# Two MLPs behind a gated linear recurrence on one core: splits and scans of the opening in another order, w_g and w_u split by ScalarE, b2 two rounds later

## What is computed

```python
t   = rmsnorm(x, norm1_w)
xb  = causal_depthwise_conv(t @ Wx, conv_w, conv_b)      # 4 taps
r, i = sigmoid(xb @ Wa), sigmoid(xb @ Wi)
a   = exp(-8 * softplus(lam) * r)
h_t = a_t * h_(t-1) + sqrt(max(1 - a_t**2, 1e-12)) * (i_t * xb_t)
h1  = x + (h * gelu(t @ Wy)) @ Wo
u   = rmsnorm(h1, norm2_w)
y   = h1 + (gelu(u @ Wg) * (u @ Wu)) @ Wd                # hidden size 1024
x1  = layernorm(x + y)
out = layernorm(x1 + relu(x1 @ W1 + b1) @ W2 + b2)       # hidden size 1024
```

## Time and profile before

| | us |
|---|---|
| three runs | 639.7, 638.1, 639.01; median 639.01 |
| profiled execution | 639.91 |
| its span, first to last instruction | 638.0 |
| TensorE busy | 606.2 (95%) |
| VectorE busy | 385.0 (60%) |
| ScalarE busy | 301.6 (47%) |
| GpSimd busy | 213.5 (33%) |
| HBM traffic | 15.7 MB, mean 25 GB/s |

### The profile page before, as it was taken

How to read it: one execution, slowest core, us unless ns; L and a number is a source line. 1 busy time by engine, 2 the same in 40 slices (tenths; PEclk the granted TensorE clock), 3 DMA queues, 4 the chain that set the end, 5 groups by cost and what they waited for, 6 DMA issues and landing times.

```text
span 638.0 us, 9412 instructions
## 1 busy us (share of the span) xinstructions
PE 606.2 (95%) x3621; PEld 538.6 (84%) x3621; DVE 385.0 (60%) x689; ACT 301.6 (47%) x560; POOL 213.5 (33%) x309
## 2 busy tenths in 40 slices
PE   8888788899999999999999999999999999999994
PEld 7787676778988888888988888888988889988884
DVE  3984883936467563857467563856467464653544
ACT  5665513427544564437544564437544563332341
POOL 4604326411353207341353207340353205420311
PEclk9989889979999999999999999999999999999998
DMA  8600000000000100001010100001000100010010
GB/s 267 219 2 33 1 2 1 33 0 2 2 34 0 34 1 14 21 1 34 1 34 1 34 1 9 25 1 34 2 1 1 34 1 1 1 34 2 0 34 33
DMA packets 13068, 15.68 MB, mean 25 GB/s; under 512 B 584, under 2 KB 12256, under 8 KB 13024
## 3 DMA queue, kind: packets, MB, share of 16 engines
q1 hardware_dynamic: 13024, 15.09, 7.0%
HBM read 10.89 MB, written 4.19 MB: 24 GB/s over the span
## 4 chain that ended last, share of the span: by engine, by line
PE 85%; DVE 8%; POOL 3%; issue 2%; ACT 1%; DMA 1%; POOLq 0%; ACTq 0%; DVEq 0%
PE psum L280 17%; PE psum L281 17%; PE psum L282 17%; PE psum L288 10%; PE psum L290 10%; PE psum L289 10%; PE psum L295 3%; DVE xb L720 1%; DVE gu_lo L822 1%; POOL rstd L999 1%; POOL normed L1030 1%; DVE tT_lo L709 1%; DMA xs<-in_L_attn_x_dram 1%; DVE gu_raw L817 0%; DVE x1T_lo L709 0%
## 5 line engine op out<-in xcount | busy, mean ns | idle before, releaser
L1059 POOL TENSOR_SCALAR gu_hi<-gu_raw 128x512 fp32r<-128x512 f32 x64 | 50.5, 790 | 299.2 <-DVE gu_raw L817 299.2
L827 DVE TENSOR_TENSOR hid_lo<-hid_raw,hid_hi 128x512 fp32r<-128x512 f32 x64 | 45.2, 707 | 95.1 <-ACT hid_hi L603 95.1
L599 ACT ACTIVATE hid_raw<-psum,vecs 128x512 f32<-128x512 f32 x64 | 43.9, 686 | 121.3 <-PE psum L282 121.3
L817 DVE TENSOR_TENSOR gu_raw<-psum,gu_raw 128x512 f32<-128x512 f32 x64 | 44.1, 689 | 92.7 <-PE psum L282 92.7
L590 ACT ACTIVATE gu_raw<-psum 128x512 f32<-128x512 f32 x64 | 38.3, 598 | 92.3 <-PE psum L282 91.7
L288 PE MATMUL psum<-w_d_hi,gu_hi 128*128 128x256 f32 x256 | 73.0, 285 | 5.9 <-DVE w_d_lo L838 3.5
L288 PE MATMUL psum<-w_hi,hid_hi 128*128 128x256 f32 x256 | 71.7, 280 | 1.2 <-DVE hid_lo L827 0.7
L290 PE MATMUL psum<-w_d_hi,gu_lo 128*128 128x256 f32 x256 | 72.2, 282 | 0.0
L289 PE MATMUL psum<-w_d_lo,gu_hi 128*128 128x256 f32 x256 | 72.0, 281 | 0.0
L290 PE MATMUL psum<-w_hi,hid_lo 128*128 128x256 f32 x256 | 71.8, 281 | 0.0
L289 PE MATMUL psum<-w_lo,hid_hi 128*128 128x256 f32 x256 | 71.7, 280 | 0.0
(11 more groups left out here) (145 smaller groups left out, 1548.8 us busy)
## 6 DMA issues: line engine op xcount, KB each, us to landing
xs<-in_L_attn_x_dram SPq DMA_DIRECT2D x8, 512.0 KB, 3.4
out_dram<-row SPq DMA_DIRECT2D x16, 256.0 KB, 2.2
raw<-in_L_ffn_W_dram SPq DMA_DIRECT2D x2, 1024.0 KB, 13.1
raw_gud<-in_L_attn_Wg_dram SPq DMA_DIRECT2D x1, 1024.0 KB, 9.0
raw_gud<-in_L_attn_Wu_dram SPq DMA_DIRECT2D x1, 1024.0 KB, 11.1
raw_gud<-in_L_attn_Wd_dram SPq DMA_DIRECT2D x1, 1024.0 KB, 13.2
raw_xyai<-in_L_attn_Wx_dram SPq DMA_DIRECT2D x1, 256.0 KB, 2.7
raw_xyai<-in_L_attn_Wy_dram SPq DMA_DIRECT2D x1, 256.0 KB, 3.1
```

Source lines behind the costliest of these rows:

```text
L599: nc.scalar.activation(hid_raw[:, w % SLOTS, :], bank[:, :], ACT.Relu, bias=vec("b1", m)).then_inc(relu_ready, 1)
L817: nc.vector.tensor_tensor(gu_raw[:, r % SLOTS, :], up_bank(r)[:, :], gu_raw[:, r % SLOTS, :], ALU.mult).then_inc(gu_ready, 1)
L827: nc.vector.tensor_tensor(hid_lo[:, w % SLOTS, :], hid_raw[:, w % SLOTS, :], hid_hi[:, w % SLOTS, :].bitcast(FP32), ALU.subtract).then_inc ...
L1059: nc.gpsimd.tensor_scalar(gu_hi[:, r % SLOTS, :], gu_raw[:, r % SLOTS, :], 1.0, 0.0, ALU.mult, ALU.add).then_inc(gu_hi_ready, 1)
```

## The change

It has these parts. (1) ScalarE instead of GpSimd makes the high halves of w_g (after the high half of tT(1)) and w_u (after the square root of the gate of chunk 0); it also makes those of w_1 in round 1 and of w_2 in round 3, which GpSimd made in rounds 0 to 3. (2) VectorE makes the constants from lam straight after w_x_lo; w_u_lo in one go after hy_lo(0); w_d_lo before round 0; w_1_lo in rounds 2 and 4, w_2_lo in rounds 5 and 6; chunk 1's scan at the end of round 3; the low half of uT ahead of gate_lo in m = 7; the last taps of chunk 2 in round 10 instead of 9. (3) GpSimd splits w_d only when mT_lo(0) is ready, and adds b2 after gate_hi in m = 3. (4) ScalarE squares h1 ahead of gelu_gate in m = 6. (5) The last chunk's second product goes into the bank pair DOWN, and in round 66 mlp_down comes ahead of mlp_up. (6) 24 instead of 18 filler products before the transposes of u(0).

```diff
+        def second_bank(c):
+            return DOWN if c == CHUNKS - 1 else SECOND
...
             def mlp_down(w):
                 c, m = divmod(w, KH)
                 pe.wait_ge(hid_lo_ready, w + 1)
-                if m == 0 and c >= 1:
+                if m == 0 and c == CHUNKS - 1:
+                    pe.wait_ge(s1_ready, 2 * CHUNKS)
+                elif m == 0 and c >= 1:
                     pe.wait_ge(s2_ready, 2 * c)
...
+                if r == UNITS + 2:
+
+                    mlp_down(r - LAG_DOWN)
                 if units(r - LAG_UP):
                     mlp_up(r - LAG_UP)
-                if units(r - LAG_DOWN):
+                if units(r - LAG_DOWN) and r != UNITS + 2:
                     mlp_down(r - LAG_DOWN)
...
-            keep_running(18, SECOND)
+            keep_running(24, SECOND)
```

ScalarE:

```diff
+                if mixing and m == 6:
+                    square_h1(n)
                 if units(r):
                     gelu_gate(r)
...
                     if m == 2:
                         gate_scale(n)
                         act.preload_act_table(ACT.Gelu_apprx_tanh)
+                    if m == 1:
+                        weight_hi("1")
+                    if m == 3:
+                        weight_hi("2")
                     if m == 4:
                         hy_hi(n)
...
                 if mixing:
-                    if m == 6:
-                        square_h1(n)
...
             split_hi(tT_hi, tT_done, tT_hi_ready, 1)
+            weight_hi("g", "n2")
             tanh_decay(0, bank=GATE)
...
             gate_scale(0)
             act.preload_act_table(ACT.Gelu_apprx_tanh)
+            weight_hi("u", "n2")
             hy_hi(0)
```

VectorE (the steps from `lams = ...` to `half_c` are the 15 of lam; they now stand where the first removed lines were):

```diff
-                if r == 3:
-                    scan_both(n)
...
-                gate_lo(r)
-                if r == 0:
-                    weight_lo("d")
-                if r == 1:
-                    weight_lo("1", ks=[0])
-                if r == 2:
-                    weight_lo("1", ks=[1])
-                if r == 4:
-                    weight_lo("2", ks=[0])
-                if r == 5:
-                    weight_lo("2", ks=[1])
                 if r == 7:
                     split_lo(uT_lo, uT_hi, uT_hi_ready, uT_lo_ready, n)
+                gate_lo(r)
+                if r == 2:
+                    weight_lo("1", ks=[0])
+                if r == 3:
+                    scan_both(n)
+                if r == 4:
+                    weight_lo("1", ks=[1])
+                if r == 5:
+                    weight_lo("2", ks=[0])
+                if r == 6:
+                    weight_lo("2", ks=[1])
...
+                if m == 2 and p == 1:
+                    convolve(n, 2)
...
                     if m == 1:
                         convolve(n, 1)
-                        convolve(n, 2)
+                        if p > 1:
+                            convolve(n, 2)
...
             weight_lo("x", "n1")
-            split_lo(tT_lo, tT_hi, tT_hi_ready, tT_lo_ready, 0)
-            weight_lo("y", "n1")
-            weight_lo("a")
-            weight_lo("i")
-            for step in range(LOOKBACK):
-                convolve(0, step)
-            xb_lo(0)
-            split_lo(tT_lo, tT_hi, tT_hi_ready, tT_lo_ready, 1)
...
+            split_lo(tT_lo, tT_hi, tT_hi_ready, tT_lo_ready, 0)
+            weight_lo("y", "n1")
+            weight_lo("a")
+            weight_lo("i")
+            for step in range(LOOKBACK):
+                convolve(0, step)
+            xb_lo(0)
+            split_lo(tT_lo, tT_hi, tT_hi_ready, tT_lo_ready, 1)
+
             weight_lo("g", "n2")
             weight_lo("o")
             room(0)
             gated_input(0)
-            weight_lo("u", "n2", ks=[0])
             scan_both(0)
             gated(0)
             hy_lo(0)
-            weight_lo("u", "n2", ks=[1])
+            weight_lo("u", "n2")
...
             split_lo(uT_lo, uT_hi, uT_hi_ready, uT_lo_ready, 0)
+            weight_lo("d")
```

In `round_of` of VectorE `split_lo` of uT moves ahead of `gate_lo` in m = 7 as well. GpSimd:

```diff
-                if m == 2 and first:
-                    add_b2(f)
                 if r < UNITS:
                     gate_hi(r)
-                if r < 2:
-                    weight_hi("1", ks=[r])
-                elif r < 4:
-                    weight_hi("2", ks=[r - 2])
...
+                if m == 3 and first:
+                    add_b2(f)
...
-            pool.wait_ge(taps_added, 3 * KD)
-            weight_hi("g", "n2")
-            weight_hi("u", "n2")
+            pool.wait_ge(xb_lo_ready, KD)
             weight_hi("d")
```

More of the change, by code:

```diff
@@ L414, in mlp_down @@
                 pe.wait_ge(hid_lo_ready, w + 1)
-                if m == 0 and c >= 1:
+                if m == 0 and c == CHUNKS - 1:
+                    pe.wait_ge(s1_ready, 2 * CHUNKS)
+                elif m == 0 and c >= 1:
                     pe.wait_ge(s2_ready, 2 * c)
                 for tt in range(TT):
-                    last = product_by_tokens(half_bank(SECOND, tt), "2", m, hid_hi[:, w % SLOTS, toks(tt)],
+                    last = product_by_tokens(half_bank(second_bank(c), tt), "2", m, hid_hi[:, w % SLOTS, toks(tt)],
                                              hid_lo[:, w % SLOTS, toks(tt)], m == 0 and tt % 2 == 0, m == KH - 1)
@@ L811, in second_sum @@
                     total = pair_of(rows[c % 2], q)
-                    nc.vector.tensor_tensor(total, psum[SECOND + q][:, :], total, ALU.add).then_inc(s2_ready, 1)
+                    nc.vector.tensor_tensor(total, psum[second_bank(c) + q][:, :], total,
+                                            ALU.add).then_inc(s2_ready, 1)
             def gate_times_up(r):
@@ L911, in round_of @@
                         hy_lo(n)
+                    if m == 7:
+                        split_lo(uT_lo, uT_hi, uT_hi_ready, uT_lo_ready, n)
                 if m == 3 and second:
@@ L918, in round_of @@
                         convolve(n, 1)
-                        convolve(n, 2)
+                        if p > 1:
+                            convolve(n, 2)
                     if m == 4:
                         room(n)
-                    if m == 7:
-                        split_lo(uT_lo, uT_hi, uT_hi_ready, uT_lo_ready, n)
                 if m == 0 and first:
```

## The result

Four runs of the changed kernel took 628.42, 628.22, 632.39 and 631.03 us, median 629.72; the kernel before took 639.04 beside them. The ratio is 0.986 [0.9819, 0.9901]. In a second set of five runs the same kernel had a median of 626.78 against 638.72, ratio 0.9822 [0.9798, 0.9847]. The profiled execution took 628.42 (span 626.5, mean granted clock 0.994); that of before 639.91 (638.0, 0.982). So it became faster by 9 to 12 us; the forecast was 12.6 and 626.4.

The account below looks back on a forecast made before the run. TensorE, busy at full clock from 140 to 600 us, bounds the kernel; gains lie in the first 140 and last 40. 1.95 + 3.1 + 1.7 - 0.9 + 1.5 + 1.9 + 2.7 + 0.6 = 12.6, giving 626.4; range 622.5 to 631.

Parts of the forecast that it names:

- The front, 1.95: Opening up to u(0): its transposes come 1.95 us earlier, bounds 0.5 and 2.9.
- Rival (b): More low clock behind one or two remaining waits, or slower ScalarE copies: 628.5 to 631 us; chance 0.18.
- Period 0, 3.1 + 1.7: Before down(0): moving w_d_lo shrinks the wait of 3.5 to 0.4, gaining 3.1 us, and 1.7 of clock.
- rival (a): Fewer losses: the wait before down(4) does not lower the clock, and w_2_lo lets rstd pass; 623.5 us, chance 0.17.
- normed, -0.9: Round 6, before u(1): w_2_lo's second half beside rstd makes TensorE wait 2.2 instead of 1.3, 0.9 us lost.
- uT_lo, 1.5: uT_lo(1) goes ahead of gu_lo(7): the wait of 1.6 falls to 0.1, 1.5 us gained.
- Period 1, 1.9 + 2.7: Before mlp_up(0): moved add_b2 and taps cut the 3.3 wait to 1.4, gaining 1.9 us, and 2.7 of low clock.
- ScalarE's copies: Weight copies moved to ScalarE: 1.05 us each, 2.1 a pair, fitting its idle time; nothing waits at w_2_hi.
- Steady periods, zero, and the end, 0.6: Steady periods: add_b2 fits VectorE's idle time, zero change; the end: mlp_down(56) starts 1.4 earlier, 0.6 us gained, bounds 0 and 1.6.
- Rival (d): Slower: later add_b2 collides with the path to mix_out(n) in six periods, up to 651 us; chance 0.03.
- Rival (c): VectorE bounds the opening, so removed waits return as the next late gu_lo: about 635 us; chance 0.09.
- (e): No effect: the copies on ScalarE hide behind nothing and take the gain, 639 us within 0.3%; chance 0.03.

Follow-up runs that it names:

- after: The changed kernel itself, all parts of the change, against the kernel before: first set of four runs median 629.72 us, ratio 0.986.
- a1_again: The changed kernel run again with no edit, five runs against the kernel before: median 626.78 us, ratio 0.9822.
- a2_lam_back: The changed kernel with the constants of lam back behind tT_lo(1) on VectorE: median 627.09 us, ratio 0.9812 to the kernel before.
- a6_best: The changed kernel with lam back, b2 back in round 2 save in period 1, last half of w_2_lo in round 7: median 624.8 us, ratio 0.9781.
- b3_period1: The kernel before with period 1 alone changed (chunk 2's last taps in round 10, chunk 0's b2 in round 11): median 635.69 us, ratio 0.9949.
- a4_w12_gpsimd: The changed kernel with the high halves of w_1 and w_2 made by GpSimd again in rounds 0 to 3: median 629.69 us, ratio 0.9869.
- a3_b2_back: The changed kernel with add_b2 back in round 2 ahead of gate_hi, except in period 1: median 627.09 us, ratio 0.9812.
- b2_lam_early: The kernel before with the 15 lam steps alone moved ahead of tT_lo(0): median 637.44 us, ratio 0.9979.
- b1_wd_early: The kernel before with w_d_lo alone moved ahead of round 0: median 635.77 us against 639.2, ratio 0.9944.

## Why the prediction was right, and where its terms were not

626.4 was forecast; 629.72 and 626.78 were measured in two sets of runs. Faster was right. That the second median lies so near 626.4 is in part luck: in that set's profile the front is 0.2 better than forecast and period 0 2.0 better, against 0.3 less in period 1 and 1.4 less from there to the end. Of the terms, compared by span:

- *The front, 1.95*: 0.63 in the profile of after, 2.17 in a1_again. The end of the lam chain (12.4 for 12.6), exp (28.66 for 28.8) and mT_lo (1.35 for 2.21) came out. The step that failed is "mix_decay(0) is 0.65 late (bounds: 0.9 early, 1.0 late)": it was 2.03 late in the profile of after and 0.48 in a1_again, because I gave the new wait of 1.9 at tT_lo no low clock, though the waits of 2.0 and 2.4 in the earlier trace rows had one. Rival (b) had this for other waits but not for mix_x(0), the one wait that the change adds. The sign I had set for ScalarE, a late tanh(0), was met in part: in a1_again it starts 0.83 later than before, 0.35 more than mix_decay(0), behind the two copies of w_g. The second tanh still waits for TensorE, so this cost nothing that the trace shows.
- *Period 0, 3.1 + 1.7*: measured 7.30 - 0.63 = 6.7. The wait before down(0) is 0.55 for 0.4, and its clock is 1.00. The rest, 6.7 - 2.95 - 1.7 = 2.0, lies at gu_lo, for which I had "zero gained": its wait is 1.8, forecast 2.5 and 2.4 before, and the low clock behind it did not come. The clock is the first half of rival (a). In a2_lam_back and a6_best the same wait was followed by the low level, so (a) and the forecast are both seen here, one execution at a time. (The price in (a) has a slip: it adds 1.2 for w_2_lo, where the sum had taken off only 0.9, so it should say 623.8.)
- *normed, -0.9*: 2.2 for 1.3, by w_2_lo beside the power of rstd (1.87 for 1.02). As forecast. The Trainium skill, page "SBUF — State Buffer", section "Who interferes with whom", says that the port pair is locked for a whole instruction; the 1.87 agrees: w_2_lo's half, 1.22 long, began at 93.11, 0.22 ahead of the power.
- *uT_lo, 1.5*: 7.98 - 6.47 = 1.5. As forecast.
- *Period 1, 1.9 + 2.7*: 12.24 - 7.98 = 4.3, and 4.3 alone in b3_period1. The wait gave 3.3 - 1.2 = 2.1, and the other 2.2 is the clock, for 2.7.
- *ScalarE's copies*: pairs take 2.19 scaled and 2.00 plain, forecast 2.1; no gelu entered TensorE's waits. a4_w12_gpsimd puts the pair w_1 and w_2 at 1.7 of waits, with up to 1.2 of clock on top. What the pair w_g and w_u is worth alone was not measured.
- *Steady periods, zero, and the end, 0.6*: 0.0 for the six full periods, -0.4 in period 7 and -0.35 at the end. The step that failed is "add_b2's new place is behind rstd of the second norm, where VectorE idles". In the full periods it holds; in the last two it does not: it meets the normalising of rows and a hid_lo, 0.4 in period 7 and 0.9 at the end (a3_b2_back against a1_again). The size of the end itself, 0.55, was right once b2 is out of its way. Rival (d) had b2 collide with the path to mix_out in the six full periods, at 25 us; the collision came on other work, only where the mix part is missing, and cost 1.3.

Rival (c) is excluded by the sum up to 124 us, (d) and (e) by the time. Rival (b), low clock behind waits that remain, gave 628.5 to 631, and the first set's median lies there; its mechanism is what was seen, but in the one execution with a trace the low stretch stood behind mix_x(0), which (b) does not list. The medians of the two sets differ by 3 us and the first set reached 632.4. This goes with the mean clock (0.985 to 0.994 in the first set, 0.993 to 0.997 in the second): what remains of waits near 2 us is followed by a low stretch in some executions. The Trainium skill, page "TensorE: Matmul & The Clock Gate", Part 1, says that the monitor runs free of the kernel; the traces agree, with the same wait of 1.8 before down(4) at 1.00 in one execution and at 0.72 in another.

## What to carry to other kernels

A wait of about 2 us on TensorE has two prices, its own length and, in some executions, a low stretch behind it, 1.5 to 2.2 us here; so compare profiles position by position at the same clock, and put filler products into the waits that can't be removed, ahead of the semaphore and not behind it. A GpSimd pass over SBUF that is moved into an idle place of VectorE must be looked up in the first and last periods too, where other work is missing and the engines stand otherwise. Undo single parts of a change that won: here two of its moves, lam early and b2 later outside period 1, cost 1.4 and 1.3. And don't take the worth of a part from one kernel to the other: lam early alone gained 1.8 on the kernel before.

## What the hardware showed that I had not expected

- One wait, two outcomes. Before mix_x(0): 1.9 us (after) and 2.0 us (b2_lam_early) were followed by 0.59 and 0.53, but 2.0 us (a3_b2_back) and 2.2 us (a1_again) by 1.00. Before u(0): 1.9 us by 1.00 in a1_again and by 0.68 in a6_best. Before down(4): 1.8 us by 1.00 and by 0.72. In the kernel before, before mix_out(0): 2.0 us by 0.57, but 2.1 us (b1_wd_early) by 1.00. Between 1.8 and 2.3 us length did not decide.
- Filler in the waits, together with lam moved back, narrowed five runs from 1.8 us (626.48 to 628.26) to 0.14. The filler alone left one run of five 1.6 above the others.
- Two-element steps on VectorE took 0.39 each beside GpSimd's passes and 0.19 alone, so a chain that is tiny by its work was 1.4 us longer (seven steps, 2.72 for 1.33).
